# A three-layer SAGE network on one core: the first layer's layer norm moves from the rows to the products

## The chip, the cores and the metric

The kernel runs on one core of a Trainium2 chip. The metric is the device time in microseconds (us) of one execution, lower is better. Before the change the median of three runs is 1517.98 us (1517.83 to 1520.94).

## The reference

```python
def _layernorm(x, eps=1e-5): return (x - mean(x)) / sqrt(var(x) + eps)     # along a row
def _sage_conv(x, src, dst, Wp, bp, Wl, bl, Wr):
    h = relu(x @ Wp.T + bp)
    agg = segment_sum(h[src], dst, N) / max(count(dst), 1)[:, None]
    return agg @ Wl.T + bl + x @ Wr.T
def _relu_ln(x, g, b): return layernorm(relu(x)) * g + b

h0 = relu(_layernorm(x))
h1 = _relu_ln(_sage_conv(h0, ...W0), g0, be0)
h2 = _relu_ln(_sage_conv(h1, ...W1), g1, be1)
out = x + _sage_conv(h2, ...W2)
```

`x` is 10000 x 512 float32, there are 5000 edges sorted by `dst`, and each of the three layers has three 512 x 512 weights.

## The kernel before, in words

**Tiles and products.** The 10000 nodes are 79 tiles of 128 rows. Each float32 operand of a product is split in a high part of type float32r and the low rest, and a product is three matmuls (low x high, high x low, high x high) for each of K = 4 chunks of 128: twelve matmuls of 512 columns for a node tile (`r_product`, lines 732 to 740). The 5000 edges are 40 tiles of 125 rows in ten groups of four; a group takes four projections (`project`, twelve matmuls of 500 columns each) and four edge products (`edge_product`, twelve matmuls each).

**The stages of a layer.** First a node loop of steps i = -9 to 71 (79 in the last layer), in which step i multiplies node tile i by Wr; then the edge loop of steps s = 0 to 39. In the first two layers the last 8 of the 79 node tiles are "late": they are normalised in the node loop with the others, are turned in the last four edge steps, and are multiplied at the start of the next layer.

**One node tile in the first layer.** SyncE (SP) loads the rows (`rows_in`, a ring of 8). VectorE (DVE) takes `bn_stats`, `bn_aggr`, a reciprocal and an offset (lines 1073 to 1088); ScalarE (ACT) takes the root (951) and writes the normalised row tile `xn` (961, a ring of 4), which SP stores to `node_x` in memory for the gathers of the edge stage (496). TensorE (PE) turns `xn` with four transposes of 128 columns (`turn`, 724) into one of two PSUM banks; ACT reads the bank and writes the high part with the ReLU (`node_xt_high`, 927), DVE the low part (`xt_low_of`, 1047); PE multiplies; DVE adds the bias (`node_out`, 1103), and SP stores the result to `node_z` (483).

**The order of work is written out by hand.** Every engine has one instruction list, and in step i it does its share for tiles ahead of i: 8, 7 and 6 for the statistics, 5 for `xn`, 2 for the turn and the split. Lists are strictly in order, so a wait holds all that is behind it. `LATER` shifts the work ahead of the product in the first layer by two steps.

**Beside the first layer's products** the edges are sorted: SP loads five key tables of 500 KB each in steps 1 to 5 (452) and Wp, 1 MB, in step 1; GpSimd (POOL) makes one-hot masks; PE counts (`count`, 2 narrow bf16 matmuls a step from step 3) and looks up (`lookup`, 4 a step from step 27); DVE ranks one tile a step from step 5 (`rank`, 1143, over 500 columns) and reads the lookups (1222). Wp is split in steps 8 to 11, Wl in steps 30 to 33 (ACT and DVE, ACT and POOL). SP writes zeros, 2 MB, in step 20. The sorted `src` is there from step 61 (`edges_in_order`), and POOL gathers edge rows from `node_x` (594) once all `xn` tiles are stored; each gathered tile is turned by PE and split as the node tiles are, and the first six are turned in steps 68 to 70.

## Time and profile before

| what | value |
|---|---|
| median of three runs | 1517.98 us |
| the profiled execution | 1517.14 us, its span 1515.0 us |
| TensorE's granted clock over the span | 0.998 |
| first layer: node loop, edge loop | about 0 to 262 us, 262 to 495 us |
| memory traffic | 291.72 MB, mean 193 GB/s |

The span runs from the first to the last instruction of the profiled execution; 2.1 us of its own time lie around it. Busy times of matmuls are modelled with their latency and overlap, so a matmul of 390 ns is followed by the next one after 230 ns: what a matmul costs is read from the distance of two starts.

### The profile page before, as it was taken

Reading aid. Unit: us, or ns where it says so; the run is one execution under the profiler, and the core shown is the slowest. Engines: PE = TensorE matmul, PEld = TensorE weight load, DVE = VectorE, ACT = ScalarE, POOL = GpSimd, SP = SyncE. Lnnn points to the kernel's source line nnn. Section 1 sums busy time; section 2 is a strip of 40 time slices with the busy share of each in tenths; the row PEclk is TensorE's granted clock in tenths of the full one; section 3 lists DMA queues with packets and bytes.
Section 4 is the critical chain, followed back from the end, with each engine's and each line's share of the span. In section 5 each row is a group of like instructions: output and inputs, shape, how many; then the busy total and the mean of one; then the engine's idle time right before and its main releaser. Section 6 shows DMA issues by size and latency. Waiting matters only on the chain.

```text
span 1515.0 us, 21400 instructions
## 1 busy us (share of the span) xinstructions
PE 1492.6 (99%) x7295; PEld 1221.5 (81%) x7295; DVE 981.2 (65%) x2164; ACT 687.1 (45%) x1267; POOL 578.6 (38%) x534
## 2 busy tenths in 40 slices
PE   7999999999999999999999999999999999999997
PEld 5787887888888888888888888888888888888886
DVE  7999975655555687777565655557766666555552
ACT  5545452232233577767322323357676652322322
POOL 4737754344323100100434442323354366444323
PEclk9999999999999999999999999999999999999999
DMA  8897877555554878887645555489999986455434
GB/s 301 319 377 249 271 249 238 111 90 89 93 85 56 242 263 306 271 275 253 216 108 90 88 93 88 54 244 320 345 329 324 328 292 207 80 89 90 73 45 60
DMA packets 152855, 291.72 MB, mean 193 GB/s; under 512 B 19885, under 2 KB 19948, under 8 KB 152620
## 3 DMA queue, kind: packets, MB, share of 16 engines
q1 hardware_dynamic: 123708, 224.81, 43.3%
q0 software_dynamic: 28464, 64.51, 24.7%
q8 instruction: 59, 0.97, 0.3%
q10 hardware_dynamic: 576, 1.05, 0.2%
q14 instruction: 48, 0.39, 0.1%
HBM read 132.33 MB, written 157.92 MB: 192 GB/s over the span
## 4 chain that ended last, share of the span: by engine, by line
PE 89%; DMA 4%; DVE 3%; issue 2%; POOL 1%; ACT 1%; SPq 0%; POOLq 0%; ACTq 0%; DVEq 0%
PE bank L737 12%; PE bank L736 12%; PE bank L738 12%; PE bank L724 9%; PE bank L820 7%; PE bank L822 7%; PE bank L821 7%; PE bank L841 7%; PE bank L843 7%; PE bank L842 7%; DMA node_x<-xn 2%; DVE stats L1073 1%; DVE rows_out L1103 1%; DVE h_low L1047 1%; DMA rows_in<-node_x,sorted_src 1%
## 5 line engine op out<-in xcount | busy, mean ns | idle before, releaser
L736 PE MATMUL bank<-w_high,h_low 128*128 128x512 f32 x900 | 374.6, 416 | 0.0
L737 PE MATMUL bank<-w_low,h_high 128*128 128x512 f32 x900 | 356.3, 396 | 0.0
L738 PE MATMUL bank<-w_high,h_high 128*128 128x512 f32 x900 | 354.5, 394 | 0.0
L981 ACT ACTIVATE h_high<-h_pre 128x500 fp32r<-128x500 f32 x120 | 74.6, 622 | 449.0 <-DVE h_pre L1284 449.0
L594 POOL DMA_INDIRECT rows_in<-node_x,sorted_src x120 | 124.1, 1034 | 274.6 <-PE bank L724 199.8
L927 ACT ACTIVATE h_high<-bank 128x512 fp32r<-128x512 f32 x221 | 131.4, 595 | 155.2 <-PE bank L724 155.0
L738 PEld LDWEIGHTS bank<-w_high,h_high 128*128 128x128 f32 x900 | 169.3, 188 | 40.3
L1050 DVE TENSOR_TENSOR h_low<-bank,h_high 128x512 fp32r<-128x512 f32 x152 | 105.0, 692 | 146.4 <-ACT h_high L927 144.5
L961 ACT ACTIVATE xn<-rows_in,off,rstd 128x512 f32<-128x512 f32 x237 | 189.4, 806 | 13.6 <-issue 9.0
L820 PE MATMUL bank<-xt_low,w_high 128*128 128x500 f32 x480 | 194.5, 405 | 0.0
L736 PEld LDWEIGHTS bank<-w_high,h_low 128*128 128x128 f32 x900 | 169.8, 189 | 30.3
L737 PEld LDWEIGHTS bank<-w_low,h_high 128*128 128x128 f32 x900 | 170.2, 189 | 29.5
L841 PE MATMUL bank<-w_high,h_low 128*125 128x512 f32 x480 | 190.1, 396 | 0.7 <-DVE h_low L1290 0.7
L843 PE MATMUL bank<-w_high,h_high 128*125 128x512 f32 x480 | 189.4, 395 | 0.0
L842 PE MATMUL bank<-w_low,h_high 128*125 128x512 f32 x480 | 189.1, 394 | 0.0
L621 POOL DMA_INDIRECT node_z<-rows_out,into_i x80 | 126.5, 1581 | 156.4 <-ACT rows_out L992 123.1
L822 PE MATMUL bank<-xt_high,w_low 128*128 128x500 f32 x480 | 186.2, 388 | 0.0
L821 PE MATMUL bank<-xt_high,w_high 128*128 128x500 f32 x480 | 185.9, 387 | 0.0
L1275 DVE TENSOR_SCALAR h_pre<-bank,bias_p 128x500 f32<-128x500 f32 x120 | 88.6, 739 | 149.5 <-PE bank L822 149.0
L1073 DVE BATCH_NORM_STATS2 stats<-rows_in 128x6 f32<-128x512 f32 x237 | 160.5, 683 | 6.8 <-DMA rows_in<-x 6.7
L612 POOL TENSOR_TENSOR residual<-residual,bias_z 128x512 f32<-128x512 f32 x79 | 102.5, 1297 | 150.3 <-DMA residual<-x 150.1
L1284 DVE TENSOR_TENSOR_SCAN h_pre<-carry,h_pre 128x500 f32<-128x500 bf16 x120 | 143.9, 1199 | 3.8
(127 smaller groups left out, 2209.1 us busy)
## 6 DMA issues: line engine op xcount, KB each, us to landing
node_x<-xn SPq DMA_DIRECT2D x237, 256.0 KB, 3.9
rows_in<-node_z SPq DMA_DIRECT2D x158, 256.0 KB, 4.4
node_z<-rows_out SPq DMA_DIRECT2D x142, 256.0 KB, 2.8
out<-rows_out SPq DMA_DIRECT2D x79, 256.0 KB, 3.5
rows_in<-x SPq DMA_DIRECT2D x78, 256.0 KB, 4.6
residual<-x SPq DMA_DIRECT2D x78, 256.0 KB, 4.3
node_z<-bias_z SPq DMA_DIRECT2D x16, 256.0 KB, 3.6
rows_in<-node_x SPq DMA_DIRECT2D x16, 256.0 KB, 2.6
```

What stands on the lines that cost most here:

```text
L736: nc.tensor.matmul(psum, low[:, k, :], w_high("r", l)[:, k, :], start=(k == 0), stop=False)
L737: nc.tensor.matmul(psum, high[:, k, :], w_low("r", l)[:, k, :], start=False, stop=False)
L738: last = nc.tensor.matmul(psum, high[:, k, :], w_high("r", l)[:, k, :], start=False, stop=(k == K - 1))
L820: nc.tensor.matmul(psum, w_high("p", l)[:, k, cols], low[:, k, :], start=(k == 0), stop=False)
L821: nc.tensor.matmul(psum, w_high("p", l)[:, k, cols], high[:, k, :], start=False, stop=False)
L822: last = nc.tensor.matmul(psum, w_low("p", l)[:, k, cols], high[:, k, :], start=False, stop=(k == K - 1))
L841: nc.tensor.matmul(psum, low, w_high("l", l)[:, m, :], start=(m == 0), stop=False)
L842: nc.tensor.matmul(psum, high, w_low("l", l)[:, m, :], start=False, stop=False)
L843: last = nc.tensor.matmul(psum, high, w_high("l", l)[:, m, :], start=False, stop=(m == K - 1))
L961: S.activation(xn[:, to, :], rows_in[:, slot, :], ACT.Identity, bias=off[:, slot:slot + 1], scale=rstd[:, slot:slot + 1]).then_inc(n_xn, 1)
L1073: V.bn_stats(stats[:, slot, :], rows_in[:, slot, :]).then_inc(n_stats, 1)
L1284: V.tensor_tensor_scan(h_pre[:, m % 2, :], carry[:, g * GROUP:(g + 1) * GROUP, :].rearrange("p t e -> p (t e)"), h_pre[:, m % 2, :], 0.0, ...
```

## The change

In the first layer's node loop nothing is normalised and nothing is turned. The host hands over a second copy of `x`, `x_t`, in which each block of 128 rows is already turned. For each tile SP loads the row tile (`rows_in`) and the turned tile (into the ring of four that was `xn`, `load_turned`). ACT sums a row tile into `minus_mean` and its squares into `spread` (two wide activations with an accumulator), and makes the high part of a diagonal matrix of `minus_mean`; DVE makes the low part; PE multiplies a matrix of ones by both (`spread_mean`: two float32r matmuls of 128 columns in place of four transposes), which puts the mean of each row along a row of PSUM; DVE adds it to the turned tile in place (`centre`), ACT and DVE split as before but from SBUF, PE multiplies, and `node_out` multiplies the product's row by one over the root and adds the bias in one instruction. The root is taken for four tiles at once. `node_x` is not written in this layer; POOL gathers from `x`, and each of the 40 gathered edge tiles is normalised in place, with the statistics that nodes had (steps 63 to 70 for tiles 0 to 7, then in the edge loop). Late tiles are loaded from `x_t` and have their spread after the edge product of their step.

Also: ranks 16 to 39 go from DVE to ACT; the counts are spread over steps 5 to 20 (40 of them, as before), the lookups start at step 25 and the sorted order is read at step 60; `LATER` goes; Wr's chunks are split one a step; the carry's table is written only once all squares are taken (`spread_carry`, ahead of POOL's ninth gather).

```diff
+AHEAD_SUM = 5
+AHEAD_DIAG = 4
+AHEAD_SPREAD = 3
+AHEAD_SPLIT = 2
+AHEAD_SQUARE = 3
+EARLY = 2
+AHEAD_LOAD_T = 5
+DIAGS = 3
-R_CHUNKS = {-4: (0,), -3: (1, 2), -2: (3,)}
+R_CHUNKS = {-5: (0,), -4: (1,), -3: (2,), -2: (3,)}
-STEP_COUNT = 3
-COUNTS = 2
+STEP_COUNT = 5
+COUNTS = 5
+RANKS_DVE = 16
-STEP_LOOKUP = 27
+STEP_LOOKUP = 25
-STEP_SORTED = 61
+STEP_SORTED = 60
+STEP_EDGE_NORM = 63
...
+        def first_at(i, ahead):
+            return [t for t in (i + ahead, i + ahead + 1) if 0 <= t < product_count[0]
+                    and t - ahead - (1 if t < EARLY else 0) == i]
...
+            def load_turned(t):
+                slot = t % XN_RING
+                if t >= XN_RING:
+                    sp.wait_ge(xt_low_done, node_no(0, t - XN_RING) + 1)
+                sp.dma_start(xn[:, slot, :], x_t[t * P:(t + 1) * P, :]).then_inc(t_loaded[slot], DMA)
...
+                    if l == 0 and XN_RING <= i + AHEAD_LOAD_T < product_count[0]:
+                        load_turned(i + AHEAD_LOAD_T)
...
+                elif l == 0:
+                    last = NODE_TILES - 1
+                    pool.wait_ge(n_square, last - (last - t) % IN_RING + 1)
                 G.indirect_dma_start(
-                    out=rows_in[:, slot, :], out_offset=None, in_=node_x,
+                    out=rows_in[:, slot, :], out_offset=None, in_=node_x if l else x_in,
...
+            def spread_mean(c, d):
+                if c == 0:
+                    pe.wait_ge(ones_done, 2)
+                if c >= 2:
+                    pe.wait_ge(xt_low_done, c - 1)
+                pe.wait_ge(n_diag_low, d + 1)
+                psum, slot = bank[c % 2][:, 0:P], d % DIAGS
+                nc.tensor.matmul(psum, ones_r[:], diag_low[:, slot, :], start=True, stop=False)
+                nc.tensor.matmul(psum, ones_r[:], diag_high[:, slot, :], start=False, stop=True).then_inc(turned, 1)
...
+            def sum_of(u):
+                S.activation(beside[:, 0, :], rows_in[:, slot, :], ACT.Identity, scale=-1.0 / D,
+                             accum_out=minus_mean[:, t:t + 1]).then_inc(n_sum, 1)
+            def square_of(u):
+                S.activation(beside[:, 1, :], rows_in[:, slot, :], ACT.Square, bias=minus_mean[:, t:t + 1],
+                             accum_out=spread[:, t:t + 1]).then_inc(n_square, 1)
+            def diag_high_of(t):
+                S.activation(diag_high[:, t % DIAGS, :], ident[:], ACT.Identity, scale=minus_mean[:, t:t + 1]
+                             ).then_inc(n_diag_high, 1)
+            def first_xt_high(t):
+                S.activation(node_xt(True, t), xn[:, t % XN_RING, :], ACT.Relu).then_inc(xt_high_done, 1)
...
+            def diag_low_of(t):
+                dve.wait_ge(n_diag_high, t + 1)
+                V.scalar_tensor_tensor(out=diag_low[:, t % DIAGS, :], in0=ident[:], scalar=minus_mean[:, t:t + 1],
+                                       in1=diag_high[:, t % DIAGS, :].bitcast(F32), op0=ALU.mult, op1=ALU.subtract
+                                       ).then_inc(n_diag_low, 1)
+            def centre(c, rows):
+                dve.wait_ge(turned, c + 1)
+                x = rows.rearrange("p (k m) -> p k m", k=K)
+                mean_row = bank[c % 2][:, 0:P].rearrange("p (a m) -> p a m", a=1).to_broadcast([P, K, P])
+                V.tensor_tensor(x, x, mean_row, ALU.add).then_inc(n_centred, 1)
...
+                elif l == 0:
+                    dve.wait_ge(n_scale, scale_no(t))
+                    V.scalar_tensor_tensor(out=rows_out[:, slot, :], in0=bank[4 + t % 4][:],
+                                           scalar=spread[:, t:t + 1], in1=bias_z[:], op0=ALU.mult, op1=ALU.add
+                                           ).then_inc(n_out, 1)
...
+                    else:
+                        for cols in scales_at(i - 1 + AHEAD_SQUARE):
+                            scale_of(cols)
+                        if is_product(l, i - 1):
+                            node_out(l, i - 1)
+                        for t in first_at(i, AHEAD_SPREAD):
+                            node_centre(t)
+                        for t in first_at(i, AHEAD_SPLIT):
+                            node_xt_low(l, t)
+                        for t in first_at(i, AHEAD_DIAG):
+                            diag_low_of(t)
```

## Rows read from the trace of the kernel before

**Rows 1.** The page: busy time of the engines, share of the span, instructions

```profile
PE 1492.6 (99%) x7295; PEld 1221.5 (81%) x7295; DVE 981.2 (65%) x2164; ACT 687.1 (45%) x1267; POOL 578.6 (38%) x534
```

**Rows 2.** Stretches of the first layer: length, busy by engine, clock, DMA share, GB/s

```profile
0.00:20.00 20.00, 9.64 (x38) 7.64 (x39) 13.54 (x40) 11.96 (x23) 3.74 (x22) 1.00 0.79 279
30.00:40.00 10.00, 10.00 (x55) 7.89 (x54) 7.13 (x21) 5.11 (x11) 7.01 (x12) 1.00 1.04 408
...
120.00:150.00 30.00, 29.77 (x174) 24.70 (x175) 29.93 (x115) 15.21 (x31) 23.93 (x31) 1.00 0.75 246
...
240.00:260.00 20.00, 18.81 (x101) 15.31 (x100) 8.51 (x14) 4.52 (x8) 12.49 (x13) 1.00 0.79 251
260.00:480.00 220.00, 220.00 (x1033) 180.66 (x1032) 128.28 (x157) 64.94 (x109) 84.27 (x62) 1.00 0.52 93
```

**Rows 3.** PE in order of time, one plain step: start, length, instruction

```profile
20.64 0.60 PE L724 MATMUL bank<-ident,xn 128*128 128x128 f32 x4
21.00 0.48 PE L736 MATMUL bank<-w_high,h_low 128*128 128x512 f32 x1
21.31 0.40 PE L737 MATMUL bank<-w_low,h_high 128*128 128x512 f32 x1
...
23.87 0.60 PE L724 MATMUL bank<-ident,xn 128*128 128x128 f32 x4
```

**Rows 4.** PE in order of time: narrow matmuls beside turns

```profile
30.45 0.28 PE L765 MATMUL bank<-shift_sum 128*128 128x128 bf16 x2
30.58 0.61 PE L724 MATMUL bank<-ident,xn 128*128 128x128 f32 x4
...
98.12 0.38 PE L771 MATMUL bank<-residual,step_down 128*128 128x128 f32 x2
98.34 0.60 PE L724 MATMUL bank<-ident,xn 128*128 128x128 f32 x4
```

**Rows 5.** PE in order of time: the first product, its end, and the next

```profile
10.83 0.78 PE L736 MATMUL bank<-w_high,h_low 128*128 128x512 f32 x1
...
15.37 0.60 PE L724 MATMUL bank<-ident,xn 128*128 128x128 f32 x4
...
17.77 0.48 PE L736 MATMUL bank<-w_high,h_low 128*128 128x512 f32 x1
```

**Rows 6.** PE in order of time: two lookups that waited

```profile
116.07 0.42 PE L789 MATMUL bank<-residual,h_pre 128*125 128x128 bf16 x4 [0.98 <-DVE unread L1222]
...
120.23 0.42 PE L789 MATMUL bank<-residual,h_pre 128*125 128x128 bf16 x4 [0.48 <-DVE unread L1222]
```

**Rows 7.** DVE groups by line and shape: count, busy us, mean ns, idle before

```profile
L1073 DVE BATCH_NORM_STATS2 stats<-rows_in 128x6 f32<-128x512 f32 x237 | 160.5, 683 | 6.8 <-DMA rows_in<-x 6.7
L1103 DVE TENSOR_TENSOR rows_out<-bank,bias_z 128x512 f32<-128x512 f32 x142 | 96.7, 681 | 0.0
L1143 DVE TENSOR_SCALAR_CACHE_REDUCE unused<-key_row,key_f 125x500 bf16<-125x500 f32 x40 | 28.7, 718 | 0.0
L1171 DVE TENSOR_TENSOR step_down<-ident,step_down 128x128 f32<-128x128 f32 x1 | 0.3, 284 | 0.0
```

**Rows 8.** ACT groups by line and shape

```profile
L946 ACT ACTIVATE rows_in<-rows_in 128x512 f32<-128x512 f32 x158 | 97.8, 624 | 20.4 <-DMA rows_in<-node_z 19.3 <-POOL rows_in L604 1.0
L951 ACT ACTIVATE std<-mean,eps 128x1 f32<-128x1 f32 x237 | 67.4, 291 | 109.9 <-DVE mean L1078 109.6
L904 ACT ACTIVATE w_high<-stage,gain 128x512 fp32r<-128x512 f32 x8 | 5.9, 733 | 0.0
```

**Rows 9.** DMA issues of 20 to 30, 30 to 40, 90 to 100, 150 to 200 us: us to landing

```profile
rows_in<-x SPq DMA_DIRECT2D x4, 256.0 KB, 7.0
...
rows_in<-x SPq DMA_DIRECT2D x3, 256.0 KB, 9.8
...
rows_in<-x SPq DMA_DIRECT2D x4, 256.0 KB, 9.6
...
rows_in<-x SPq DMA_DIRECT2D x17, 256.0 KB, 3.4
```

351 lines of the change are left out of this document (261 added, 90 removed).

## The prediction

> **What bounds the kernel now.** I read the page first for the busy times. TensorE (PE) is busy for 99% of the span and VectorE (DVE) for 65% [rows 1], so time comes off only where PE gets less to do or where it waits. Then I read the stretches of the first layer, which alone is changed. PE has 10.4 us idle in the first 20 us, 0.2 in 120 to 150, 1.2 in 240 to 260, and none in the 220 us of edge work from 260 to 480. Two numbers there warn. DVE is busy for 29.93 of 30 us in 120 to 150, so that stretch is on the edge of being DVE's. And from 30 to 40 us the DMA engines are full, at 408 GB/s [rows 2]. The clock is 1.00 throughout, so no term below comes from it. Last I read PE in order of time, for what a step is made of. A plain step goes from turn to turn, 20.64 to 23.87 us, 3.23 us. Its turn holds PE for 0.36 us up to the first matmul of the product. That matmul is followed after 0.31 us, while the other eleven come every 0.233 us ((23.87 - 21.31) / 11). So a turn costs 0.36 + 0.08 = **0.44 us**, and the twelve matmuls 2.79 [rows 3].
>
> **The change, part by part.** The sum is made against the profiled execution, 1517.14 us; the median of the runs, 1517.98, is 0.84 above it.
>
> *Spread in place of turn, 71 tiles.* Two float32r matmuls of 128 columns replace four float32 transposes. No row of before has a float32r matmul that narrow. The nearest is the one float32 product of 128 columns, which runs as two passes of 128 x 128 and holds PE from 98.12 to 98.34: 0.11 us a pass [rows 4]. The cheap bound is the pair of bf16 matmuls of 128 columns, 30.45 to 30.58, 0.065 us each [rows 4]. The dear bound is that a narrow float32r matmul takes as long as a wide one, 0.233 [rows 3]. I take 0.11, since operands, shape and weight load are nearest. A spread is then 2 x 0.11 + 0.08 for the slow first matmul behind it = 0.30, and saves 0.14: 71 x 0.14 = **-9.9**. With the cheap bound it is 0.21, saving 16.3; with the dear one 0.47 (nothing is left to add behind it), losing 2.1.
>
> The Trainium skill ("TensorE: Matmul & The Clock Gate", section "Back-to-back issue gap") measured about 81 ns for each matmul of 128 columns in a stream of loads and matmuls. By that a spread is 0.24 and the term would be -14.2 in place of -9.9. The same passage gives 131 ns at 512 columns where this trace has 233, so I let the row decide.
>
> *Late tiles.* Four pairs of turns become four pairs of spreads in the edge loop: eight transposes are at least 8 x 0.09 + 0.08 = 0.80, four narrow matmuls 0.52. **-1.1** (bounds -1.8 and +0.5). Behind each stand DVE's two centres and the splits. They have an edge product of 2.8 us as cover, and without it each pair would cost some 2 us.
>
> *The start.* Before, product 0 ran from 10.83 to 15.37, and product 1 began only at 17.77, because a turn between them waited for ACT [rows 5]; product 2 began at 21.00 [rows 3]. Now product 0 also stands behind tile 2's spread in PE's list. ACT's share before it is two sums, one square, three diagonals, three chunks of Wr and two splits, so I put it at 11.5 or so; but products 0 and 1 stand side by side. 11.5 + 4.5 + 0.3 + 2.8 + 0.4 = 19.5 for product 2: **-1.5** (bounds -3 and +3, since tiles 2 and 3 are loaded behind the graph's).
>
> *VectorE in a step.* Removed: statistics 0.68 and three small ones. Added: centre, like the bias addition that also reads PSUM, 0.68, and the low diagonal, like a 128-column operation, 0.28 [rows 7]. That is equal within 0.2 us, so the step needs about 2.3 us (bias, centre, split 0.68 each, diagonal 0.28), 3.1 with a rank of 0.72, under the new step of 3.09 + counts 0.16. From step 21 the ranks are ACT's, and the lookups no longer meet them. The two lookups for which PE waited, 0.98 and 0.48 [rows 6], go: **-1.5** (bounds -1.5 and 0).
>
> *ScalarE in a step.* Before: one normalisation, a root, a split. Now a sum 0.62, a square with one pointer 0.73, a diagonal at most 0.3 to 0.4, a split 0.62 [rows 8]: 2.3 of 3.09 us, and in steps 21 to 39 + 5 a rank of 0.73 more: 3.05. That is cover that just suffices while accumulators cost nothing to read. No row shows one on ACT; the bounds are 0 and the smallest ACT instruction, 0.29 [rows 8]. On DVE the read of the accumulator hides under the next instruction, so I take 0 and keep the other end as a rival.
>
> *Loads of turned tiles.* The bytes are the same (a load of 256 KB for a store). But a store of `xn` was waited for by no product, and now the load stands on the path of its own tile. Slot t is asked for by SP behind `node_out(t - 6)` of DVE, and DVE's centre waits for it with all its list behind it: the next `node_out`, the splits, and `diag_low`, for which PE's next spread waits. Going round: landing, then split 0.68, diagonal 0.28, rank 0.72, the next `node_out` 0.68, SP's issues 0.5, and the load again, once every three steps. So a step is at least (landing + 2.9) / 3, and it binds above a landing of 3 x 3.25 - 2.9 = 6.9 us. Later in the loop loads land in 3.4 us. Where key tables and Wp share the queue they took 7.0 and 9.8 us, and beside the zeros 9.6 [rows 9]. At 9.8 the step is 4.2, 0.97 over. I take three such steps less 0.9 of slack, and two beside the zeros at 0.83: 2.0 + 1.7 = **+3.7** (bounds 0 and +16, twelve and five steps). DVE finds its data late first; PE is late a step behind.
>
> *Into the edges.* Gathers no longer wait for the last store of `xn`; PE's 1.2 us idle in 240 to 260 [rows 2] goes: **-1.2** (bounds -1.2 and +2, as statistics of gathered tiles now stand in DVE's list, some two steps behind their gather).
>
> *Edge loop.* 40 edge tiles add about 1.2 us of DVE (statistics 0.68 and small ones) and 1.1 of ACT each. DVE was busy for 128 of 220 us there and ACT for 65 [rows 2]; with some 45 more both stay under PE: 0. The gather is three tiles ahead. Were this cover gone, each tile would cost up to its 1.2 us. Counts, lookups, Wr's order and the roots (one small pair in four steps): 0.
>
> Sum: -9.9 - 1.1 - 1.5 - 1.5 + 3.7 - 1.2 = -11.5, so 1505.6 for a profiled execution and **1506.5** for the median.
>
> **The rivals.**
> *Narrow is as dear as wide.* If a float32r matmul of 128 columns takes 0.23 us, the two first terms become +2.1 and +0.5, and all is 2.1: 1520. For it: nothing in the trace shows the narrow form to be cheap, and a float32 pass is a different mode. Against it: the float32 pass of the same 128 columns takes half of that [rows 4].
> *The loads set the pace (slower).* In both full stretches the landing stays near 9.8 us for twelve and five steps: 12 x 0.97 + 5 x 0.83 = 15.8, and the gains at the start and at the lookups vanish, since DVE is what is late: -9.9 - 1.1 - 1.2 + 15.8 = +3.6, 1521.6. It decides from a landing of 6.9 us held for some fifteen steps. For it: DMA is full at 408 GB/s. Against it: a loop that waits asks for less, and the queue empties.
> *ScalarE becomes the bound.* With 0.2 to 0.29 for each accumulator, steps 21 to 44 have 3.3 to 3.6 us of ACT beside splits of Wl and the late tiles, against 3.09 + 0.23: about +6 on the sum, 1512.5. For it: 3.05 of 3.3 us is already taken.
> *The normalised edge rows hold PE* at the turn of the stages, or the change saves nothing net for a cause not listed: within 3 us of 1518.
>
> **How the numbers follow.** Forecast 0.51, narrow as wide 0.16, loads 0.13, ScalarE 0.12, the last 0.08. All terms at the good end give -22, 1496; the range keeps most of the cheap bound's side and reaches to the rivals at 1520 and 1521.6, of whose upper halves some is left out: 1498 to 1521. A measurement of this kernel can tell about 0.2%, 3 us. The forecast and ScalarE are faster; narrow-as-wide and the last case mostly the same with a part on each side; loads mostly slower: faster 0.70, same 0.17, slower 0.13.
>
> **What would show it.** Right: PE's starts from spread to product 0.22 apart, a plain step of 3.09 where it was 3.23; product 2 before 20 us; no idle lookup; ACT busy for over 80% of steps 21 to 44 with PE not waiting. Wrong: starts of the two narrow matmuls 0.2 or more apart; DVE idle before the centre for `x_t` over many steps; PE idle before a spread with ACT full; or idle before edge turns for `n_xn`.

## The result, and the profile after

The changed kernel takes 1534.19 us (median of four runs, 1532.52 to 1536.32) beside 1517.90 us for the kernel before: a ratio of 1.0101, 95% interval 1.0088 to 1.0113. That is 16 us slower, where 11.5 us faster was predicted, and it lies outside the range of 1498 to 1521. The profiled execution has a span of 1531.9 us, 16.9 more than before, at a mean granted clock of 0.995.

The first lines are the page's busy times, then the same stretches as in [rows 2], in the same columns.

```profile
PE 1486.3 (97%) x7137; PEld 1211.8 (79%) x7137; DVE 1025.1 (67%) x2140; ACT 804.2 (53%) x1651; POOL 587.7 (38%) x535
```

```profile
0.00:20.00 20.00, 8.77 (x28) 7.07 (x29) 9.68 (x19) 15.39 (x39) 4.31 (x23) 1.00 0.88 293
20.00:30.00 10.00, 8.19 (x33) 6.55 (x32) 8.33 (x26) 6.39 (x18) 4.91 (x8) 0.83 0.85 251
30.00:40.00 10.00, 7.17 (x30) 5.55 (x29) 4.99 (x11) 5.03 (x15) 0.00 (x0) 0.91 1.05 406
120.00:150.00 30.00, 29.26 (x161) 24.06 (x160) 25.87 (x81) 29.34 (x81) 23.61 (x29) 1.00 0.80 248
210.00:240.00 30.00, 25.11 (x110) 20.14 (x109) 24.12 (x46) 18.08 (x50) 9.58 (x10) 0.94 0.69 220
240.00:260.00 20.00, 17.31 (x79) 13.28 (x79) 16.48 (x42) 14.53 (x35) 5.38 (x7) 1.00 0.58 176
260.00:480.00 220.00, 217.69 (x1031) 178.43 (x1030) 163.75 (x297) 98.77 (x178) 86.02 (x66) 1.00 0.52 102
```

PE has 6 us less to do than in [rows 1], and the span is 17 us longer: PE waits. In 120 to 150 us ACT has taken DVE's place as the full engine, and PE still works 29.26 of 30. The losses are elsewhere: in 30 to 40 us, where DMA is full and DVE works for half of the time; in 210 to 240, where the DMA engines are not full; in 240 to 260; and 2.3 us in the edge loop, where before PE had no idle time. In three stretches the clock is under 1.00, which it was in none of [rows 2].

Next, PE in order of time: one plain step, to be laid beside [rows 3].

```profile
30.84 0.22 PE L828 MATMUL bank<-h_low,ones_r 128*128 128x128 f32 x1
30.90 0.28 PE L829 MATMUL bank<-h_high,ones_r 128*128 128x128 f32 x1
31.01 0.45 PE L840 MATMUL bank<-w_high,h_low 128*128 128x512 f32 x1
31.30 0.39 PE L841 MATMUL bank<-w_low,h_high 128*128 128x512 f32 x1
31.53 0.39 PE L842 MATMUL bank<-w_high,h_high 128*128 128x512 f32 x1
```

A narrow float32r matmul is followed after 0.06 us, the second after 0.11, and the spread costs 0.17 up to the product and 0.06 more for the slow first matmul behind it: 0.23. The gain that was hoped for is there, and larger. (Where a step also has four lookup matmuls, the two of the spread take 0.14 and 0.12, at 128.17 to 128.43 us for example, so the gain is smaller there.) To see where the rest goes, I took the start of each product from PE's rows and cut the span there. The last two columns are versions run below.

| stretch, us | before | after | four edits + spread loads | before + spread loads |
|---|---|---|---|---|
| start to product 3 | 24.22 | 28.01 | 28.72 | 23.56 |
| products 3 to 25 | 74.48 | 80.66 | 73.36 | 73.88 |
| products 25 to 50 | 87.28 | 81.78 | 81.72 | 85.18 |
| products 50 to 70 | 67.11 | 71.84 | 63.22 | 67.65 |
| product 70 to edge product 0 | 19.03 | 20.65 | 20.66 | 19.02 |
| edge product 0 to late product 0 | 223.35 | 227.61 | 225.45 | 223.35 |
| late product 0 to late product 7 | 20.62 | 21.74 | 21.73 | 20.62 |
| from there to the end | 998.91 | 999.61 | 999.14 | 998.94 |

Only the 25 products from 25 to 50 run about as forecast. Three places cost most. The first is where DMA is full. These are the rows of DVE; the number in brackets is its wait ahead of the instruction, with what ended it.

```profile
31.05 0.75 DVE L1353 SCALAR_TENSOR_TENSOR rows_out<-bank,spread,bias_z 128x512 f32<-128x512 f32 x1 [0.89 <-PE bank L842]
35.14 0.69 DVE L1278 TENSOR_TENSOR xn<-xn,bank 128x512 f32<-128x512 f32 x1 [3.34 <-DMA xn<-x_t]
```

In 20 to 40 us the turned tiles land after 9.2 us (median of five issues). Over the whole node loop the waits of the centre for them add up to 9.1 us, in four waits of 3.34, 0.64, 2.90 and 2.22 us. The third ended at 92.12 us, just as the zeros were being asked for (91.17 to 94.86), so what it stood beside is Wl's 1 MB, asked for at 82.79:

```profile
xn<-x_t SPq DMA_DIRECT2D x5, 256.0 KB, 9.2
```

```profile
L1278 DVE TENSOR_TENSOR xn<-xn,bank 128x512 f32<-128x512 f32 x71 | 48.2, 678 | 13.1 <-DMA xn<-x_t 9.1 <-PE bank L829 4.0
```

The second place I had not thought of. It is at step 57, with DVE, POOL and PE in order of time:

```profile
212.75 0.68 DVE L1251 SCALAR_TENSOR_TENSOR h_low<-xn,h_high 128x512 fp32r<-128x512 f32 x1
213.35 5.37 DVE L1269 SCALAR_TENSOR_TENSOR h_low<-ident,minus_mean,h_high 128x128 fp32r<-128x128 f32 x1
218.65 0.74 DVE L1353 SCALAR_TENSOR_TENSOR rows_out<-bank,spread,bias_z 128x512 f32<-128x512 f32 x1
```

```profile
213.62 4.94 POOL L671 TENSOR_TENSOR w_low<-stage,w_high 128x512 fp32r<-128x512 f32 x4
```

```profile
218.87 0.30 PE L828 MATMUL bank<-h_low,ones_r 128*128 128x128 f32 x1 [4.42 <-DVE h_low L1269]
219.00 0.30 PE L829 MATMUL bank<-h_high,ones_r 128*128 128x128 f32 x1
219.15 0.77 PE L840 MATMUL bank<-w_high,h_low 128*128 128x512 f32 x1
219.72 0.63 PE L841 MATMUL bank<-w_low,h_high 128*128 128x512 f32 x1
220.14 0.63 PE L842 MATMUL bank<-w_high,h_high 128*128 128x512 f32 x1
```

The low diagonal, 0.34 us elsewhere, takes 5.37 us and ends when POOL's four splits of Wl end. Behind the gap of 4.42 us PE is granted the lower of its two levels (1.2 GHz) for a while (0.64 on average from 219.0 to 223.7 us): its matmuls start 0.43 apart and not 0.23, 1.6 us for that step. Steps 2 and 5 have the same, 4.57 and 4.81 us where 3.00 and 3.24 would be plain. (Product 0's matmuls start 0.43 apart too, in both kernels, though the granted clock is recorded as 1.00 there.) But the length of a gap does not tell it. The clock fell behind the first of these two gaps and stayed behind the second:

```profile
23.19 0.30 PE L828 MATMUL bank<-h_low,ones_r 128*128 128x128 f32 x1 [1.81 <-DVE h_low L1269]
...
93.82 0.30 PE L828 MATMUL bank<-h_low,ones_r 128*128 128x128 f32 x1 [2.02 <-DVE h_low L1269]
```

The third place is steps 64 to 66, 3.62, 3.99 and 3.96 us. Here DVE waits in the middle of its list:

```profile
242.64 0.69 DVE L1313 BATCH_NORM_STATS2 stats<-rows_in 128x6 f32<-128x512 f32 x1
243.36 0.18 DVE L1317 BATCH_NORM_AGGREGATE mean<-stats 128x2 f32<-128x6 f32 x1
243.91 0.17 DVE L1321 RECIPROCAL rstd<-std 128x1 f32<-128x1 f32 x1 [0.36 <-ACT std L1127]
244.11 0.21 DVE L1325 TENSOR_SCALAR off<-mean,rstd 128x1 f32<-128x1 f32 x1
```

### The profile page after: what moved, and what is told of

Its sections match the earlier page's. It is cut to its first block, busy times and chain, and to the rows that moved or that the text cites. A ratio compares the mean times of both kernels' runs of the same rounds, so it can differ in the third digit from the quotient of the medians.

```text
span 1531.9 us, 21684 instructions
## 1 busy us (share of the span) xinstructions
PE 1486.3 (97%) x7137; PEld 1211.8 (79%) x7137; DVE 1025.1 (67%) x2140; ACT 804.2 (53%) x1651; POOL 587.7 (38%) x535
## 4 chain that ended last, share of the span: by engine, by line
PE 84%; DVE 5%; DMA 4%; issue 3%; ACT 3%; POOL 1%; POOLq 0%; SPq 0%; DVEq 0%; ACTq 0%
PE bank L840 12%; PE bank L841 11%; PE bank L842 11%; PE bank L817 7%; PE bank L951 7%; PE bank L953 7%; PE bank L952 7%; PE bank L930 7%; PE bank L932 7%; PE bank L931 7%; DMA xn<-x_t 2%; DVE h_low L1251 1%; DVE h_low L1269 1%; DVE xn L1278 1%; DMA rows_in<-x,sorted_src 1%
## 5 line engine op out<-in xcount | busy, mean ns | idle before, releaser
L952 PE MATMUL bank<-w_low,h_high 128*125 128x512 f32 x480 | 189.0, 394 | 0.0
L682 POOL DMA_INDIRECT rows_in<-node_x,sorted_src x80 | 82.6, 1032 | 193.9 <-PE bank L817 132.4
L1102 ACT ACTIVATE h_high<-bank 128x512 fp32r<-128x512 f32 x150 | 89.6, 597 | 125.5 <-PE bank L817 125.5
L1313 DVE BATCH_NORM_STATS2 stats<-rows_in 128x6 f32<-128x512 f32 x198 | 134.5, 684 | 2.8 <-ACT rows_in L1123 1.9
L1548 DVE TENSOR_TENSOR h_low<-h_pre,h_high 128x500 fp32r<-128x500 f32 x120 | 81.5, 679 | 74.8 <-ACT h_high L1157 74.3
```

The source lines that it names most:

```text
L952: nc.tensor.matmul(psum, high, w_low("l", l)[:, m, :], start=False, stop=False)
L1313: V.bn_stats(stats[:, slot, :], rows_in[:, slot, :]).then_inc(n_stats, 1)
```

## The experiments

Sixteen kernels ran in four groups, each group on one chip with the kernel before beside it, which took 1517.65, 1527.68, 1517.51 and 1526.63 us. So times are compared within a group, as ratios, and where a group has no unedited changed kernel the stretches of the traces decide. In the first group "the changed kernel" is the measurement above, 1534.19 us; measured again in the third group it took 1532.37, so of such a difference some 2 us can be chance.

### First group: the two large losses, and whether the second is a matter of place

**Wl split by DVE.** POOL's four splits go, and DVE takes one in each of steps 50 to 53.

```diff
             for k in range(K):
-                split_l(0, k)
...
+                    if l == 0 and 0 <= i - STEP_LOW_L < K:
+                        low_of("l", 0, i - STEP_LOW_L)
```

> The changed kernel, but the first layer's Wl is split by VectorE in steps 50 to 53 and not by GpSimd's four subtractions. Theory: VectorE's low diagonal of step 57, two SBUF operands, took 5.37 us because GpSimd's four subtractions (4.94 us) held an SBUF port that both use; with them gone it takes 0.35 as elsewhere, PE's 4.4 us gap and the slow matmuls behind it (1.6 us) go, and the time falls by 6 us to about 1528. Rival: the hold came from the DMA of the sorted order that GpSimd starts at the same time; then the long instruction stays and the time is 1534, or 1535 with VectorE's four extra splits.

Measured: 1525.89 us, ratio 1.0056 (1.0039 to 1.0073), 8.3 us under the changed kernel. Steps 57 and 58 are 3.01 and 2.99 where they were 7.70 and 4.57, which is 6.3 of it. The rest has nothing to do with the edit as far as the trace shows: 1.8 in products 3 to 25, whose waits for loads fell otherwise in that execution, and 0.9 between late products 0 and 7. The row that took 5.37 us is back to its usual length:

```profile
211.18 0.69 DVE L1250 SCALAR_TENSOR_TENSOR h_low<-xn,h_high 128x512 fp32r<-128x512 f32 x1
211.78 0.35 DVE L1268 SCALAR_TENSOR_TENSOR h_low<-ident,minus_mean,h_high 128x128 fp32r<-128x128 f32 x1
```

**Large loads spread out.** The parts of the key table are loaded at steps 1, 7, 13, 20 and 26, Wp at 3, and the zeros at 23, 29, 35 and 41.

```diff
-                    if l == 0 and 0 <= i - STEP_LOAD_ROWS < ROW_CHUNKS:
-                        load_rows(i - STEP_LOAD_ROWS)
+                    if l == 0 and i in LOAD_ROWS_AT:
+                        load_rows(LOAD_ROWS_AT.index(i))
...
```

> The changed kernel, with the large transfers apart: key tables at steps 1, 7, 13, 20, 26 in place of 1 to 5, Wp at step 3 in place of 1, the four stores of zeros at steps 23, 29, 35, 41 in place of all at 20. Same bytes. Theory: loads of turned tiles that land after 9 us hold VectorE's list and with it PE's spread in steps 3 to 6 and 20 to 24; spread out they land in 4 to 6 us, steps 4 and 20 fall from 6.1 and 5.4 to some 3.2, and the time falls by 5 to 8 us to 1526 to 1529. Rival: ScalarE or the order of the list holds these steps; then they stay above 4.5 and the time stays within 2 us of 1534.

Measured: 1532.87 us, ratio 1.0090 (1.0067 to 1.0112), 1.3 us under the changed kernel, which its interval does not tell from nothing. The time is the rival's, but not its cause, for step 4 is plain: the stalls moved. Step 6 is 6.5 us, and at step 20, beside Wl's 1 MB (asked for at 81.67 us), there is a wait again. The centre waited 8.8 us for `x_t` in all, against 9.1:

```profile
42.03 0.69 DVE L1279 TENSOR_TENSOR xn<-xn,bank 128x512 f32<-128x512 f32 x1 [3.88 <-DMA xn<-x_t]
...
91.58 0.69 DVE L1279 TENSOR_TENSOR xn<-xn,bank 128x512 f32<-128x512 f32 x1 [3.30 <-DMA xn<-x_t]
```

In both places one large load of 1 MB, Wp or Wl, beside the tiles' own traffic was enough to make a load of `x_t` late, so spreading them alone buys almost nothing.

**The same in the kernel before.**

> The kernel before with the same spreading of the large transfers. There no load stands on a product's path within less than several steps, and PE had no gap from 20 to 110 us but 0.3, so the theory of the loads expects nothing: 1516 to 1519. If transfers in bulk cost every version the same, this gains 5 us or more as the changed kernel does.

Measured: 1514.33 us, ratio 0.9981 (0.9971 to 0.9990). Against the expectation the kernel before gains 3.3 us: step 14 goes from 3.81 to 3.36 us, and steps 29 and 30, whose lookups waited [rows 6], from 4.64 and 4.15 to 3.44 and 3.46. So the two waits whose end I had booked as a gain of the change were the loads' own, and their end could be had without it.

**Diagonals first** in ACT's and DVE's step.

```diff
+                        for t in first_at(i, AHEAD_DIAG):
+                            diag_low_of(t)
                         for cols in scales_at(i - 1 + AHEAD_SQUARE):
                             scale_of(cols)
...
```

> The changed kernel, with the diagonal's high and low part first in ScalarE's and VectorE's share of a step, ahead of the split and the centre. Same work. Theory: what PE waits for in nearly all its gaps is the low diagonal, which stands in VectorE's list behind a centre that waits for its load; ahead of it, PE keeps one step more of slack, and the gaps in the node loop (some 14 us in steps 2 to 66 with the long one of step 57) shrink by half or more: 1525 to 1529. Rival: the two engines or the loads are late on average, not by the order of the list, and the wait only moves from the spread to the product: 1532 to 1535.

Measured: 1533.94 us, ratio 1.0106 (1.0089 to 1.0123): nothing, as the rival said. PE's gaps now end on DVE's low part of the tile (`xt_low_of`) in place of the diagonal. DVE's list as a whole is late, not one piece of it.

### Second group: the smaller losses one by one

**The load of `x_t` ahead of the store** that waits for the bias addition, in SP's list.

```diff
                 for i in node_steps(l):
+                    if l == 0 and XN_RING <= i + AHEAD_LOAD_T < product_count[0]:
+                        load_turned(i + AHEAD_LOAD_T)
                     t = i - 1
                     if is_product(l, t):
...
```

> The whole changed kernel, with one line of SP's list moved: in a node step of the first layer the load of tile i+5 of x_t is asked for ahead of the store that waits for the bias addition of product i-1, instead of behind it. Theory (a load of x_t leaves late, since its place in SP's list is behind a store that waits for VectorE, and this makes the 20 us or so of stalls at steps 4, 5, 20 and 21): each load leaves about 1.5 to 2 us earlier, the longest waits of the centre for x_t fall from 3.3 us to about 1.5, steps 4 and 5 together fall by 2 to 3 us and 20 and 21 by 2 to 3 us with the clock's part, in all -4 to -6 us: about 1529. Rival (the DMA engines are full in those stretches, so a load asked for earlier lands no earlier and only delays the others): within 1.5 us of 1534.

Measured: 1535.08 us, ratio 1.0046 (1.0031 to 1.0062). The centre's waits for `x_t` fall from 9.1 to 6.9 us; steps 4 and 5 take 4.60 and 3.66 us (6.07 and 4.81), step 20 takes 3.73 (5.38), and product 25 starts 3.5 us earlier, where 4 to 6 were expected. Step 23 keeps its 4.9 us, beside the zeros. Where in SP's list a load stands was worth over a third of the loads' cost (9.1 us by the steps, see below).

**Product 0 ahead of tile 2's spread** in PE's list, and product 1 behind the spreads of tiles 3 and 4.

```diff
-                    if l == 0 and 0 <= i < EARLY:
-                        node_product(l, i)
+                    if (l, i) == (0, -1):
+                        node_product(0, 0)
...
```

> The whole changed kernel, but product 0 stands in PE's list ahead of the spread of tile 2, and product 1 behind the spreads of tiles 3 and 4, as all later products stand. Theory (product 0 waits for ACT's work for tile 2, and VectorE then stands idle for 3 us since the spread of tile 3 is behind both): product 0 starts at about 12.3 where it was 13.04, product 2 at about 22 where it was 23.44, the gap of 1.8 us ahead of product 2 is gone: -1.5 to -3 us, about 1532. Rival (VectorE's and ScalarE's work for tiles 2 to 4 sets when the steady loop begins, whatever PE's order): product 3 starts within 0.5 us of where it did, 28.0, and the time stays within 1 us of 1534.

Measured: 1538.63 us, ratio 1.0065 (1.0047 to 1.0082). Product 0 starts at 10.69 us, as early as before, and product 3 at 29.01 where it was 28.01. The theory fails, and the rival is the nearer, though its bound was 28.5. This order of PE's list doesn't make the start earlier.

**Normalised edge tiles one step apart** (`edge_factors(edge_norms(i - 1))`, and ACT's normalisation one step later).

> The whole changed kernel, but the reciprocal and offset of a gathered edge tile stand one step later in VectorE's list than its statistics, and ScalarE's normalisation one step later too. Theory (steps 63 to 67 take 3.6 to 4.0 us since VectorE waits in each for a root that ScalarE takes behind its own work): these five steps fall to 3.1 to 3.3 each, the first projection starts about 3 us earlier, and all is about -3 us: 1531. Rival (VectorE's sum of work there, statistics 0.69, mean 0.18, product 0.74, centre 0.68, split 0.69, diagonal 0.35 and small ones, makes 3.7 by itself): less than 1 us.

Measured: 1536.33 us, ratio 1.0048 (1.0029 to 1.0066). Steps 63 to 69 take 22.9 us together where they took 25.8, 2.9 where about 3 were expected, and the wait of 0.36 us for the root is gone. The profiled execution was 8.5 us longer than the changed kernel's nevertheless. It lost 4.7 in the later layers (4.1 to 4.5 in the other traces of this group), 2.3 in products 3 to 25, and 3.5 in steps 46 and 47, which took 4.99 and 4.56 us (DVE waited there for something outside the core that the profile does not name), as in no other trace. I count the stretch, not that time.

```profile
248.46 0.69 DVE L1315 BATCH_NORM_STATS2 stats<-rows_in 128x6 f32<-128x512 f32 x1
249.18 0.18 DVE L1319 BATCH_NORM_AGGREGATE mean<-stats 128x2 f32<-128x6 f32 x1
249.28 0.13 DVE L1323 RECIPROCAL rstd<-std 128x1 f32<-128x1 f32 x1
249.45 0.21 DVE L1327 TENSOR_SCALAR off<-mean,rstd 128x1 f32<-128x1 f32 x1
```

**Late diagonals a step earlier.**

```diff
+                    for j in late_turns(l, s + 1) if l == 0 and EDGE_TILES - GROUP <= s < EDGE_TILES - 1 else ():
+                        diag_high_of(product_count[0] + j)
...
```

> The whole changed kernel, but the diagonals of a late pair of tiles are built one edge step earlier, behind the splits of the pair before, instead of in the step of their own spreads. Theory (an edge step with a late pair takes 4.4 to 4.5 us, since PE's spreads wait for diagonals that stand behind four other pieces of ScalarE's list): the gaps of 0.9 to 1.1 us in the four steps go, late product 0 starts 2.5 to 4 us earlier, all about -3.5: 1530.5. Rival (the wait only moves on to the centre and the split of the late rows behind the spread): less than 1 us.

Measured: 1535.53 us, ratio 1.0050 (1.0031 to 1.0070). From edge product 32 to late product 0 it takes 35.3 us where the changed kernel has 37.5 and the kernel before 34.5: 2.2 us, less than the 2.5 to 4 expected. The gaps of 0.9 to 1.0 us ahead of the second to fourth pair are 0.35 ahead of two of them and gone ahead of one.

### Third group: is the hold GpSimd's, and do the gains add?

**The changed kernel again**, as a mark.

> The changed kernel itself, unaltered, as the mark for the three kernels beside it. Both theories: a ratio to the kernel before of 1.010 as first measured, or a few tenths of a per cent less where the kernel before itself runs longer, as it did beside the last four kernels (1527.7 us); the holds at steps 57 and 58 and the late loads at steps 4 and 20 are there again.

Measured: 1532.37 us, ratio 1.0104 (1.0085 to 1.0123), the same. The hold sits one step later, on 58.

**POOL's splits kept apart** by a wait on the bias additions.

```diff
             for k in range(K):
+                pool.wait_ge(n_out, 58 + k)
                 split_l(0, k)
```

> The whole changed kernel, but GpSimd's four splits of Wl are held apart, one for each node step from step 58 on, by a wait on the bias additions. Theory (a GpSimd operation keeps VectorE's operations with two SBUF operands out, for as long as GpSimd's run goes on): four holds of at most 1.25 us, one a step, of which the 0.5 us of slack that VectorE has in a step of 3.0 takes a part: steps 57 to 62 lose at most 2.5 us together where 6.3 were lost, no VectorE operation there takes over 1.7 us, and all is -3.5 to -5 us against the changed kernel. Rival (the hold has its cause in what VectorE's instruction waits for, or in the records, and not in GpSimd's run): one operation of VectorE still takes 4 to 5 us.

Measured: 1529.62 us, ratio 1.0079 (1.0063 to 1.0096), 2.75 us under the mark; less than the 3.5 to 5 expected. Instead of one hold of 5 us there are three of 1.4, beside the first, second and fourth split; the third was almost over when a split of DVE came, which took 0.82. The operation alone takes 0.69 us. The first are POOL's rows, then DVE's.

```profile
213.36 1.30 POOL L671 TENSOR_TENSOR w_low<-stage,w_high 128x512 fp32r<-128x512 f32 x1 [0.29 <-DVE rows_out L1354]
216.36 1.29 POOL L671 TENSOR_TENSOR w_low<-stage,w_high 128x512 fp32r<-128x512 f32 x1 [1.70 <-DVE rows_out L1354]
219.72 1.30 POOL L671 TENSOR_TENSOR w_low<-stage,w_high 128x512 fp32r<-128x512 f32 x1 [2.07 <-DVE rows_out L1354]
224.63 1.28 POOL L671 TENSOR_TENSOR w_low<-stage,w_high 128x512 fp32r<-128x512 f32 x1 [3.60 <-DVE rows_out L1354]
```

```profile
213.79 1.42 DVE L1252 SCALAR_TENSOR_TENSOR h_low<-xn,h_high 128x512 fp32r<-128x512 f32 x1
216.79 1.42 DVE L1252 SCALAR_TENSOR_TENSOR h_low<-xn,h_high 128x512 fp32r<-128x512 f32 x1
...
225.06 1.40 DVE L1252 SCALAR_TENSOR_TENSOR h_low<-xn,h_high 128x512 fp32r<-128x512 f32 x1
```

With the split by DVE this settles it: the hold is as long as GpSimd's run of these subtractions, and breaks when the run is broken. Not every run of GpSimd does this. In the changed kernel POOL makes one-hot masks without a pause from 51.51 to 65.68 us (14.17 of 14.17), and beside them the same operations of DVE are only about 0.1 us longer (0.68 and 0.35 elsewhere), while some of the masks take 0.80 to 1.08 in place of 0.60:

```profile
56.99 0.76 DVE L1251 SCALAR_TENSOR_TENSOR h_low<-xn,h_high 128x512 fp32r<-128x512 f32 x1
57.68 0.45 DVE L1269 SCALAR_TENSOR_TENSOR h_low<-ident,minus_mean,h_high 128x128 fp32r<-128x128 f32 x1
```

In the kernel with spaced splits, steps 57 to 60 are 3.0 to 3.4 us; step 61, where the sorted order is read besides, still takes 4.88 (3.81 in the changed kernel).

**Four edits together** (Wl by DVE, loads ahead, edge tiles apart, late diagonals), and **the same with the large loads spread out**.

> The changed kernel with four of the single edits together: Wl split by VectorE in steps 50 to 53 and not by GpSimd, the load of x_t ahead of the store, normalised edge tiles a step apart, late diagonals a step earlier. Theory (each takes away a loss of its own, at its own place): their gains add, 8.3 for the split as measured, 3.4 for the loads, 2.9 for the edge tiles, 3.2 for the late ones by the traces: -17 to -18 us against the changed kernel, that is, level with the kernel before (ratio 0.997 to 1.001). Rival (a gain at one place is given back at the next, since the same two engines are late behind it): less than 12 us together, ratio above 1.002.

> The same four edits and the large loads spread out (the five parts of the key table at steps 1, 7, 13, 20 and 26, Wp at 3, the zeros at 23, 29, 35 and 41). Theory (with the loads of x_t asked for earlier, no other stretch of full DMA engines is long enough to make the centre wait): stalls of steps 4, 5 and 20 gone, another -2 to -4 us against the four edits alone: ratio 0.995 to 0.998, ahead of the kernel before. Rival (as when this was tried alone, the stall only moves to the step where the next large load stands): within 1.5 us of the four edits alone.

Measured: 1519.54 us, ratio 1.0008 (0.9999 to 1.0018), and 1514.97 us, ratio 0.9979 (0.9969 to 0.9989). The four edits take 12.8 us off the mark, between theory and rival; the ratio is inside the theory's range, since the mark itself stood lower than 1534. The spread loads, worth 1.3 us alone, are worth 4.6 once the loads of `x_t` are asked for earlier: steps 4 and 23, which the four edits left at 4.87 and 5.06 us, are 2.99 and 3.01, and of the stalls 4.20 us in step 6 and 3.79 in step 20 are left.

### Fourth group: the start and the edges

**Short sums.** Sum and square of the first four tiles go over 2 columns, so their mean and root are left out.

```diff
-                S.activation(beside[:, 0, :], rows_in[:, slot, :], ACT.Identity, scale=-1.0 / D,
+                w = 2 if u < 4 else D
+                S.activation(beside[:, 0, 0:w], rows_in[:, slot, 0:w], ACT.Identity, scale=-1.0 / D,
...
```

> The whole changed kernel, but ScalarE's sum and square of the first four node tiles go over 2 columns and not 512, so the mean and the root of these four tiles are left out of what is computed. Theory (ScalarE is full until 13 us and sets the start): each of eight operations falls from 0.52 or 0.61 effective to some 0.2, product 0 starts at about 11 where it was 13.04 and product 3 at 25.5 to 26.5 where it was 28.0; the time falls by 1.5 to 2.5 us. Rival (the start hangs on the arrival of the tiles and on the round from spread to centre to split to diagonal): product 3 within 0.5 us of 28.0.

Measured: 1536.69 us, ratio 1.0069 (1.0048 to 1.0089). ACT makes tile 2's high diagonal at 10.44 us where it was 11.36, and yet product 0 starts at 12.50 (13.04), and product 3 at 27.24 (28.01, and 27.55 in the second trace of the changed kernel). The kernel with late diagonals, whose start is the changed kernel's, has product 3 at 27.20, so what the theory gained can't be told from chance; it had asked for 25.5 to 26.5. With ACT early, DVE's list is full, from its second split of Wr at 8.45 us to 12.4 without a wait, and the diagonal stands in it at 11.54 (DVE in order of time):

```profile
11.54 0.35 DVE L1271 SCALAR_TENSOR_TENSOR h_low<-ident,minus_mean,h_high 128x128 fp32r<-128x128 f32 x1
11.80 0.69 DVE L1245 SCALAR_TENSOR_TENSOR w_low<-stage,w_high 128x512 fp32r<-128x512 f32 x1
13.35 0.69 DVE L1280 TENSOR_TENSOR xn<-xn,bank 128x512 f32<-128x512 f32 x1 [0.85 <-DMA xn<-x_t]
...
17.72 0.69 DVE L1280 TENSOR_TENSOR xn<-xn,bank 128x512 f32<-128x512 f32 x1 [2.41 <-PE bank L829]
```

The last row is what neither edit of the start changed: DVE is idle beside product 0 (2.41 us here, 3.16 in the changed kernel, 3.25 with product 0 first) until PE has done the spread behind it, and the round from spread to centre to split to diagonal begins late. The changed kernel's trace says how much hangs on it: product 1 is only 0.4 us late against the kernel before (18.20, 17.77), 2.0 more come between products 1 and 2, where PE waits 1.81 us for a low diagonal, and 1.35 in step 2, at the lower clock behind that gap. No run takes that round apart.

**Short statistics** of the gathered tiles: statistics and normalisation of the 40 edge tiles over 2 columns, left out of what is computed.

> The whole changed kernel, but the statistics and the normalisation of the gathered edge tiles of the first layer go over 2 columns and not 512, so that part is left out of what is computed. Theory (these operations cost the time at steps 63 to 69, into the edges and in the edge loop, since VectorE and ScalarE have lists in which something for PE stands behind them): steps 63 to 69 fall from 25.8 to 22.5 to 23.5 us, the way from node product 70 to edge product 0 from 20.65 to about 19.2, edge products 0 to 32 from 190.2 to about 189, in all -4.5 to -6 us: about 1527. Rival (the loss there comes with spreads and diagonals, not with the edge tiles): less than 2 us.

Measured: 1534.42 us, ratio 1.0056 (1.0040 to 1.0073). Steps 63 to 69 take 22.9 us (25.8), as with the edit of order alone. Edge products 0 to 32 take 188.9 (190.2), exactly what the kernel before has. From product 70 to edge product 0 it is 21.15 us, and in the kernel with short sums, on the same chip, 20.91: there the theory fails. So the normalisation costs 1.3 us in the edge loop and its share of steps 63 to 69, and not what is lost between product 70 and edge product 0.

**One edge tile normalised earlier**, on top of the four edits and the spread loads.

```diff
-            return [] if not 0 <= t < 2 * GROUP else [t]
+            return [] if not 0 <= t < 2 * GROUP + 1 else [t]
...
```

> The four edits and the spread loads together, and the edge tile ninth in order normalised one node step earlier, so that each later pair is one tile further ahead. Theory (the gaps of 0.5 and 1.05 us at edge products 0 and 4 come since tiles ten and eleven are normalised in the same step that turns them): the gap ahead of the first edge turn beside a product goes, -1 us against 1515, about 1514. Rival (VectorE's list between the last node product and the first edge product is full, and one statistic earlier makes the projections wait): within 0.5 us of it or slower.

**The kernel before with spread loads, again.**

> The kernel before with the large loads spread out, as run before, now beside the repaired change. Theory of the sum (what the narrow matmuls save, 16 us, is used up by VectorE's and ScalarE's longer lists at both ends of the layer and in the steps where VectorE has 3.6 us to do): level, ratio of both 0.998 within 0.001. Rival (the repaired change is ahead by itself): the kernel before with spread loads stays 2 us or more behind x18.

Measured: 1521.84 us, ratio 0.9969 (0.9960 to 0.9979), and 1522.37 us, ratio 0.9977 (0.9967 to 0.9986), both beside 1526.63. Edge products 0 to 32 are back to 189.0 us: the 1.3 us were a matter of one tile's lead. Ahead of them is a new wait: behind its last node product DVE waits 0.94 us for a gather, PE 2.62 us for the normalised tile (0.79 without this edit), and from product 70 to edge product 0 it is 23.4 us where it was 20.7. So by the traces the gain of 1.2 us in the loop is paid for there. The kernel before with spread loads has 22.3 there on this chip, where it had 19.0 in the first group, while the changed kernel's versions have 20.9 and 21.2 on this chip and 20.6 to 20.9 on the others. Here the kernel before loses 3.3 us which the changed one doesn't, and that may be one reason why the singly edited kernels of the second and fourth groups stand at 1.005 to 1.007.

```profile
254.48 0.69 DVE L1318 BATCH_NORM_STATS2 stats<-rows_in 128x6 f32<-128x512 f32 x1 [0.94 <-DMA rows_in<-x,sorted_src]
```

So there are versions of both kernels that beat the kernel before, by 0.2 to 0.3%, and the intervals of the two overlap. The repaired change and the kernel before with a few loads moved are level, as the theory of the sum had it: they are 0.5 us apart where its rival asked for 2.

## Why the prediction was wrong, point by point

The sum came to -11.5, and the span grew by 16.9. PE's own work shrank by more than forecast. What failed is the pricing of waits: two terms booked as gains came out as losses (the start, the way into the edges), the loads cost over twice their term, the edge loop's normalisation was put at nothing, and the largest loss, 6.3 us, stood in no term at all.

**Spread in place of turn, -9.9.** The mechanism was right and the size too small: a spread costs 0.23 us where I took 0.30, and the plain step is 3.00 where I forecast 3.09. If all 71 steps were plain that would be -16.3, as with the cheap bound. It is less, for the 0 of "Counts, lookups" was wrong by 2.1 us: the 20 steps with lookups fell only from 3.45 to 3.29, and the 16 with counts lie 0.19 to 0.24 above a plain step, where 20 lay 0.13 above it before. Together that is -14.2. I took the float32 pass [rows 4] as nearest, and the bf16 pair in the same group came nearer. The rule of the Trainium skill that I weighed ("TensorE: Matmul & The Clock Gate", "Back-to-back issue gap": some 81 ns for each matmul of 128 columns) gave a spread of 0.24 and was nearer than my row.

**Loads of turned tiles, +3.7.** The landing of 9.2 us was as read [rows 9], and the mechanism too. The step that failed is "three such steps" and "two beside the zeros", each a little late (and 0.83 for the latter: the sum's own formula gives 0.92 for a landing of 9.6). The delay came as single waits of up to 3.3 us, which PE felt nearly in full, once with the clock's 1.6 us on top, and one of them stood beside Wl, of which I had not thought. Steps 4, 5, 20, 23 and 24 lie 9.1 us above what the same steps take without a wait, and 7.3 of it was given back with these loads moved: products 3 to 25 take 73.36 us and not 80.66. That is over twice my figure and inside its bounds of 0 and +16.

**VectorE in a step, -1.5.** The waits for lookups went, but the kernel before loses them too once its large loads are spread out. And steps 9 to 12 take 3.42 to 3.59 us, 1.3 us more together than plain steps with counts: DVE has bias, centre, split, diagonal, rank and a quarter of Wp there, and is busy for 14.04 of 14.17 us.

```profile
51.51:65.68 14.17, 13.61 (x69) 10.19 (x68) 14.04 (x28) 11.95 (x31) 14.17 (x21) 1.00 0.81 264
```

I had summed DVE for a plain step with a rank, and not for the four with Wp's parts. The kernel before was as full there (14.00 of 14 us in 51 to 65) and still kept its 3.36 us; the changed list is some 0.2 us longer, since the bias with its scaling takes 0.74 us and not 0.68, and the split and the diagonal are about 0.1 us longer each beside the masks.

**What was missing altogether: what DVE's new instructions meet.** Before, four splits of Wl by POOL lay at 213.55 to 218.6 us and cost nothing, and I left them alone as unchanged. What changed was DVE's side: its splits and diagonals now read two tensors from SBUF, where the turned tile had come from PSUM. It cost 6.3 us with the clock, more than any term of my sum but the first. "That is equal within 0.2 us" is the step that failed: the new instructions are as long as the old ones alone, and not beside POOL. The rows of before could not show it, but one sentence of the Trainium skill could. "SBUF — State Buffer", section "SBUF: two separate sides", says that GpSimd and VectorE share one pair of ports under an exclusive lock, that a VectorE operation with two SBUF inputs takes it against a GpSimd operation that reads SBUF, and that the one that comes second waits for the whole instruction. The traces agree as far as POOL's subtractions go: operations with one SBUF tensor went on beside the same four splits in the kernel before (`bn_stats` in 0.68 us at 214.23 and 217.46), and a single split of 1.30 us, 0.43 us into its run, held one with two for 0.73 us. They add that between four such operations back to back VectorE did not get in (5.37 us beside 4.94), and that between POOL's masks it did, with a wait of about 0.1 us. That the one that starts first has the port is not to be seen in the long hold, whose record begins 0.27 us ahead of POOL's first; but starts on POOL are rough. I had looked up what an added operation costs, and not what it locks.

**Into the edges, -1.2, and edge loop, 0.** Both came out as losses: 2.9 us at steps 63 to 69, where DVE waits for a root asked for in the same step; 1.6 more than before up to edge product 0; and 1.3 in the loop. I had checked that DVE's and ACT's sums stay under PE's, which they do (163.75 and 98.77 of 220 us), and not where in each list the new pieces stand. The cause of the 1.6 is open: neither of the last runs took it away. The trace shows PE waiting 0.20 and 1.01 us there for DVE's pieces of the projected edges, where the kernel before has no wait. Open too is the cause of the 1.1 us between late products 0 and 7, for which no run was made. It is one step, late product 5 to 6, 4.22 us where it was 3.11: at 528.64 us PE waits 0.90 us for ACT's `xn`, and ACT had waited 1.27 us for POOL (0.45 before). In the trace with Wl split by DVE that wait of PE is absent.

**Late tiles, -1.1.** The spreads themselves are cheap; but edge product 32 to late product 0 takes 3.0 us longer, 2.2 of which went with an earlier diagonal. I had written that the pairs have an edge product as cover, which holds for centre and split. The diagonals have none: ACT makes them behind a chunk of the next Wr and the scaling of an edge product, in the step of their own spread.

**The start, -1.5.** It became +3.8. Product 0 starts at 13.04, not 11.5, and product 2 at 23.44, not 19.5. Two steps failed. "ACT's share before it" is 1.5 us of the miss: ACT's sums hold at most 0.5 us of that, and DVE's list, which I had not added up for the start, is as full. "Products 0 and 1 stand side by side" and the 0.4 behind them are 2.4 more, most of it a gap of 1.81 us between products 1 and 2. The lower clock behind that gap adds some 1.6 to step 2, for which the sum had nothing.

**ScalarE, 0.** An accumulator's read shows as 0.19 us, and delays the next instruction by some 0.1. ACT is busy for 29.34 of 30 us in 120 to 150, and the steps there take 3.29 us against a forecast of 3.09 + 0.23 = 3.32. From 111.96 to 138.31 us, eight such steps, PE is busy for 26.35 of 26.35 us: the cover just sufficed, save at step 34 (4.22 us), where PE waited 0.74 us for a low diagonal.

**The rivals.** None of the four was the case by itself. "The loads set the pace" named one of the right places, and at its 1521.6 was the nearest; "the edge rows hold PE" was right and priced too low. Between the forecast sum and the span lie 28.4 us. The terms above account for some 27, each as measured less its forecast: port 6.3, loads 5.4, start 5.3, late tiles and late products 5.2, steps 63 to 69 2.9, into the edges 2.8, counts and lookups 2.1, Wp's steps 1.3, edge loop 1.3, the other layers 0.7, less the 6.4 that plain spreads gave beyond forecast. The rest lies in single steps such as 34 and 61 (4.22 and 3.81 us) and was not taken apart. The range had a slip of its own: all terms at the good end give -23.8 (-16.3, -1.8, -3, -1.5, 0, -1.2), 1494 and not 1496, which changes nothing here. What the sum lacked in common is that I added busy times for each engine, and priced a wait only where I had thought of one.

## What to carry to other kernels

When an operand moves from PSUM to SBUF, ask what else uses the port that its reader now needs, over the whole stretch, even where that other work isn't touched: an unchanged run of four GpSimd subtractions cost 6 us here. When work moves between lists, a sum of busy times shows only the least it can cost; write down for every wait in a list what stands behind it, and put an answer that another engine must give a step later than its question. And before a gain is booked for a change, try its cheapest part on the old kernel: moving large loads apart was worth 3.3 us there and needed nothing else.

## What the runs showed of the hardware

A float32r matmul of 128 columns was followed after 0.06 us by another and after 0.11 by one of 512 columns (0.14 and 0.12 behind bf16 lookups), where one of 512 columns takes 0.233 from start to start. A VectorE operation on two SBUF tensors was held for a whole run of four GpSimd subtractions of 128 x 512, 5.37 us for 0.34; with one such subtraction of 1.3 us beside it, one of 0.69 took 1.42 us; beside GpSimd's one-hot masks it was about 0.1 us longer. PE's granted clock fell to the lower level after gaps of 1.81, 2.83 and 4.42 us in the changed kernel and not after one of 2.02; with the large loads spread out it stayed even after one of 3.13, at 43.86 us. A fall cost about 1.6 us in the changed kernel, and 2.5 in step 58 of the kernel with product 0 first (5.55 us, every matmul 0.43 apart). The kernel before itself took 1517.6 us in two groups and 1527 in the two others, on other chips, 0.6% apart, which is more than most of the edits are worth; with spread loads, of 7.9 us between two such traces 5.1 lie in the later layers and 3.3 on the way into the edges.
